# Splitting the down weights on ScalarE and VectorE instead of GpSimd in a nine-expert MoE kernel

## The reference, cut to what matters

```python
# x: 16 sequences x 128 tokens x 128 features, float32
def moe(h, gates, sg):                    # E=8 routed experts, F=512
    g = einsum('bsd,edf->ebsf', h, Wg)
    u = einsum('bsd,edf->ebsf', h, Wu)
    outs = einsum('ebsf,efd->ebsd', silu(g) * u, Wd)
    routed = einsum('be,ebsd->bsd', gates, outs)
    shared = (silu(h @ Sg) * (h @ Su)) @ Sd
    return (1 - sg) * routed + sg * shared
x = x + moe(x, ...)
x = x + layernorm(x + adapter(x, language)) * gamma[language] + beta[language]
```

## Time and profile before

| | us |
|---|---|
| median of three runs | 326.66 |
| fastest of them | 325.96 |
| span of the profiled execution (first to last instruction) | 324.8 |
| PE busy | 305.9 |
| DVE busy | 272.0 |
| ACT busy | 218.9 |
| POOL busy | 49.5 |

### The profile page before, as it was taken

The page is one execution under the profiler, slowest core; times in us unless marked ns, Lnnn a source line. Parts: engine busy times, 40 slices in busy tenths (PEclk is TensorE's granted clock), DMA queues, the critical chain, the costliest instruction groups (busy, mean ns, idle before and its releaser), DMA issues.

```text
span 324.8 us, 6936 instructions
## 1 busy us (share of the span) xinstructions
PE 305.9 (94%) x1397; PEld 139.4 (43%) x1397; DVE 272.0 (84%) x544; ACT 218.9 (67%) x471; POOL 49.5 (15%) x51
## 2 busy tenths in 40 slices
PE   5693969999999999999999999999999999999995
PEld 1231324444445444444445444444445444444443
DVE  3999999999986788898986788898986788898864
ACT  4573647888877677777777677777767677777540
POOL 2888894000001000000001000000001000100001
PEclk9799789999999999999999999999999999999996
DMA  6990233200000000000000000000000000000000
GB/s 209 414 387 13 38 80 77 69 0 2 1 0 0 14 4 0 0 1 0 0 32 0 12 4 0 0 0 0 0 32 1 12 4 0 1 0 0 0 32 32
DMA packets 9082, 11.97 MB, mean 37 GB/s; under 512 B 3810, under 2 KB 6770, under 8 KB 9074
## 3 DMA queue, kind: packets, MB, share of 16 engines
q1 hardware_dynamic: 8784, 11.68, 10.8%
q10 hardware_dynamic: 290, 0.20, 0.2%
HBM read 10.83 MB, written 1.05 MB: 37 GB/s over the span
## 4 chain that ended last, share of the span: by engine, by line
PE 85%; DVE 1%; issue 0%; DVEq 0%
PE moe_ps L272 9%; PE moe_ps L270 9%; PE moe_ps L269 9%; PE up_ps L227 9%; PE gate_ps L227 9%; PE up_ps L228 9%; PE up_ps L229 9%; PE gate_ps L228 9%; PE gate_ps L229 9%; PE back_ps L296 1%; PE adapt_ps L280 1%; PE x_ps L366 1%; PE x_ps L288 1%; PE x_ps L364 0%; DVE gx_lo L470 0%; PE gate_ps L357 0%
## 5 line engine op out<-in xcount | busy, mean ns | idle before, releaser
L391 ACT ACTIVATE silu<-gate_ps 128x512 f32<-128x512 f32 x144 | 85.7, 595 | 70.9 <-PE gate_ps L229 70.8
L487 DVE SCALAR_TENSOR_TENSOR hidden<-silu,up_ps 128x512 f32<-128x512 f32 x144 | 98.7, 685 | 36.5 <-PE up_ps L229 18.7
L493 DVE TENSOR_TENSOR h_lo<-hidden,h_hi 128x512 f16<-128x512 f32 x144 | 101.0, 702 | 0.1
L398 ACT ACTIVATE h_hi<-hidden 128x512 f16<-128x512 f32 x144 | 89.6, 622 | 15.6 <-DVE hidden L487 15.5
L227 PE MATMUL up_ps<-gx_hi,w_hi 128*128 (+1 forms) x142 | 54.5, 384 | 9.6 <-DVE gx_lo L470 7.0
L470 DVE SCALAR_TENSOR_TENSOR gx_lo<-x_full,coef,gx_hi 128x128 f32 (+3 forms) x144 | 57.4, 421 | 0.0
L272 PE MATMUL moe_ps<-h_lo,w_hi 128*128 128x512 f16 x144 | 55.1, 383 | 0.0
L270 PE MATMUL moe_ps<-h_hi,w_lo 128*128 128x512 f16 x144 | 55.1, 383 | 0.0
L269 PE MATMUL moe_ps<-h_hi,w_hi 128*128 128x512 f16 x144 | 55.0, 382 | 0.0
L227 PE MATMUL gate_ps<-x_hi,w_hi 128*128 (+1 forms) x142 | 54.6, 385 | 0.0
L228 PE MATMUL up_ps<-gx_lo,w_hi 128*128 (+1 forms) x142 | 54.5, 384 | 0.0
(11 more groups left out here) (90 smaller groups left out, 202.3 us busy)
## 6 DMA issues: line engine op xcount, KB each, us to landing
w_full<-weights SPq DMA_DIRECT2D x8, 768.0 KB, 13.3
affine_sb<-affine SPq DMA_DIRECT2D x16, 128.0 KB, 3.0
w_full<-weights SPq DMA_DIRECT2D x3, 256.0 KB, 5.5
x_full<-xT SPq DMA_DIRECT2D x1, 768.0 KB, 8.7
out_dram<-result SPq DMA_DIRECT2D x3, 256.0 KB, 2.1
w2b_sb<-w2b SPq DMA_DIRECT2D x16, 16.5 KB
x_full<-xT SPq DMA_DIRECT2D x1, 256.0 KB, 4.7
w_sb<-w SPq DMA_DIRECT2D x16, 16.0 KB
```

Of the source, the lines that this page charges most:

```text
L391: nc.scalar.activation(cols(silu, f % 2, N), gate_ps[f % 2][:, :], ACT.Silu, scale=1.0 / W_SCALE).then_inc(silu_ready, 1)
L398: nc.scalar.activation(cols(h_hi, f, N), cols(hidden, f % 2, N), ACT.Copy).then_inc(h_hi_ready, 1)
L487: nc.vector.scalar_tensor_tensor(out=cols(hidden, f % 2, N), in0=cols(silu, f % 2, N), scalar=HIDDEN_RESCALE, in1=up_ps[f % 2][:, :], op0= ...
L493: nc.vector.tensor_tensor(cols(h_lo, f, N), cols(hidden, f % 2, N), cols(h_hi, f, N), ALU.subtract).then_inc(h_lo_ready, 1)
```

## The change

ScalarE makes the high half and VectorE the low half of the down weights too, in the step f=2 of the expert ahead (`f < 3`), and those of expert 0 ahead of the first step. GpSimd's part and its two buffers go. The counts of the semaphores `w_hi_ready` and `w_lo_ready` go from two to three for an expert. The loads, TensorE's order and everything after tile 0 stay.

```diff
--- before.py
+++ after.py
-        down64 = sb("down64", [P, F], F32)
-        w_scale = sb("w_scale", [P, F], F32)
...
@@ gate_up, down (PE)
-                    pe.wait_ge(w_lo_ready, 2 * e + 1)
+                    pe.wait_ge(w_lo_ready, 3 * e + 1)
...
-                    pe.wait_ge(w_lo_ready, 2 * e + 2)
+                    pe.wait_ge(w_lo_ready, 3 * e + 2)
...
-                    pe.wait_ge(w_down_ready, e + 1)
+                    pe.wait_ge(w_lo_ready, 3 * e + 3)
@@ expert (ACT)
-                    if next_w is not None and f < 2:
+                    if next_w is not None and f < 3:
                         if f == 0:
                             act.wait_ge(experts_loaded, next_w)
                         weight_hi(next_w, f)
...
             act.wait_ge(w0_loaded[1], 16)
             weight_hi(0, 1)
+            act.wait_ge(w0_loaded[2], 16)
+            weight_hi(0, 2)
             expert(0, 0, True, 1, None)
@@ weight_lo, expert (DVE)
-                dve.wait_ge(w_hi_ready, 2 * e + third + 1)
+                dve.wait_ge(w_hi_ready, 3 * e + third + 1)
...
-                    if next_w is not None and f < 2:
+                    if next_w is not None and f < 3:
                         weight_lo(next_w, f)
...
             weight_lo(0, 1)
+            weight_lo(0, 2)
             for q in range(BATCHES):
                 gated_x_lo(0, 1, q)
@@ (POOL)
-            nc.gpsimd.memset(w_scale[:, :], W_SCALE).then_inc(w_scale_ready, 1)
...
-            def down_weight_parts(e):
...
-            pool.wait_ge(w_scale_ready, 1)
-            pool.wait_ge(w0_loaded[2], 16)
-            down_weight_parts(0)
-            with pool.Fori(1, NE) as e:
-                pool.wait_ge(experts_loaded, e)
-                pool.wait_ge(w_down_ready, e)
-                down_weight_parts(e)
             pool.wait_ge(x_rest_loaded, 16)
```

More of the change, by code:

```diff
@@ L120, in build @@
         warm_ready = sem("warm_ready")
[L121 to L124, removed]
         w0_loaded = [sem(f"w0_loaded{i}") for i in range(3)]
```

## The result

The changed kernel takes 314.38 us (median, 314.03 to 314.89) against 326.66 us of before; the ratio is 0.962, 95% interval 0.960 to 0.964, so 3.8% faster. A fourth execution of before took 644.2 us and is left out as an outlier. The prediction was 314.5. The profiled execution took 314.35 us with a span of 312.5, 12.3 less than before.

The account below looks back on a forecast made before the run. Tile 0 was taken as short of VectorE, later tiles of TensorE. 11.5 + 6.2 + 23.6 + 2.3 = 43.6 to expert 4; 0.4 lost after left 12.2 us gained: span 312.6, plus 1.86 gives 314.5 us, range 311.0 to 319.5.

Parts of the forecast that it names:

- The start: Beginning of tile 0: first `hidden` of expert 0 at 11.5 instead of 14.21, a gain of 2.7 us.
- Expert 0 to 3: VectorE in tile 0: 6.2 us for expert 0, then three experts at 7.88, together 23.6 us.
- the input split: GpSimd's conversions for tiles 1 to 3, moving from 45 us to about 11.8, still cost a full VectorE 2.3 us.
- The upper bound of 5.5: Most that GpSimd's input conversions could cost, in us, if they block all of VectorE's work.
- The third split: VectorE's added `w_lo` in each expert of the loop: 0.60 us, bounds 0.55 and 1.65.
- The period of 7.88: VectorE's us per expert in the loop: 7.14 busy, 0.14 for the branch, and the third `w_lo`; TensorE needs 7.77.
- PE waits these 0.1 us at f=0: Experts 4 to 7: PE waits for the last `gx_lo`, pushed back by the new `w_lo`; 0.4 us lost in all.
- C: Rival, tile 0: VectorE's long instructions have another cause than GpSimd and stay long; slower, 333.7 us; chance 0.03.
- A: Rival, tile 0: TensorE's clock drops again, three unhidden slow stretches cost 4.5 us; 319.0 us; chance 0.16.
- B: Rival, tile 0: VectorE's 7.88 is too high and PE runs through without a wait; 311.4 us; chance 0.07.
- to the letter: Port lock read strictly: all of GpSimd's input conversions stand in VectorE's way, 3.2 us more than the sum.

Follow-up runs that it names:

- the run without any split: Changed kernel with no split of the down weights on any engine, TensorE multiplying by the up weights in their place: 312.52 us.
- memsets: Changed kernel with nine rounds of seven write-only memsets on GpSimd ahead of its input split: 315.41 us, from 313.65 to 317.05.
- GpSimd's rounds: Changed kernel with GpSimd's old nine rounds on the down weights added, into spare buffers that nobody reads: 333.40 us.
- the best kernel: Changed kernel with third `w_lo` behind last `gx_lo`, tile 1's inputs split after the last weights, tiles 2 and 3's in tile 1: 311.26 us.
- the three runs on it: Changed kernel with GpSimd's old rounds added (333.40 us), with memsets in their place (315.41 us), with one-input casts in their place (326.79 us).
- late inputs: Changed kernel with GpSimd's split of the input of tiles 1 to 3 held back until VectorE's last low half of the weights: 312.09 us.

## Why the prediction was right, and which term was not

**What bounds the kernel** was right: only tile 0 changed, by 12.5 us at its end (95.25 to 82.77), and the later tiles kept their 216.0 us.

**The start** came out as walked: forecast 11.5, measured 11.49. The added split of expert 0 pushed ScalarE's second four `gx_hi` to 9.92, and VectorE's new `w_lo` lay in the wait for them: without both, in the run without any split, these `gx_hi` start at 9.51 and the first `hidden` at 11.08, each 0.41 earlier.

**Expert 0 to 3**: forecast for the three experts of the loop 23.6 us, measured 23.64 (19.72 to 43.36). Expert 0 with the input split was put at 6.2 + 2.3 = 8.5 and took 8.23; without it 6.12 (memsets). So the split costs 2.1 there, not 2.3; at 45 us in the memset run it costs 2.3. The upper bound of 5.5, in which every conversion stands fully in VectorE's way, was far off. The timeline shows why: beside the conversions three `w_lo` and three `h_lo` take 0.87 to 1.09 us where 0.68 is their length alone, which is 2.1 us in all, and each `hidden` between them keeps its 0.68.

**The third split** was priced at 0.60 and cost that: VectorE's busy time for an expert went from 7.14 to 7.74 us.

**The period of 7.88** was right as a number and wrong in its reason. The step that failed is the one that took 0.14 us between experts for the branch, as time "in which VectorE waits for nobody". Some 0.1 of it is a wait for TensorE's up product, which itself waits for the last `gx_lo`; moving the third `w_lo` behind that `gx_lo` took it away with the loop's branch still there (a gap of 0.03). The kernel before had the same wait in the very gap that was read as the branch:

```profile
54.61 0.34 DVE L470 SCALAR_TENSOR_TENSOR gx_lo<-x_full,coef,gx_hi 128x128 f32 x1
```

```profile
55.33 0.39 PE L227 MATMUL up_ps<-gx_hi,w_hi 128*128 x1
...
55.77 0.38 PE L229 MATMUL up_ps<-gx_hi,w_lo 128*128 x1
```

The third pass ends at 56.15 and the `hidden` of the earlier trace rows starts at 56.29, 0.14 later, just as 35.48 is 0.14 after 35.34 in the changed kernel. So the gap that was added to the sum held a wait that comes back after the change; that it kept its length made the number right, which is luck. Hence also the slip in "PE waits these 0.1 us at f=0": true, but VectorE then waits for PE in turn. The same edit, which by my sum would win nothing in the loop, won 1.2 us of last `hidden`: about 0.1 in each expert of the loop, and 0.6 once, TensorE's wait near 26 us, which fell from 1.54 to 0.94. VectorE's landmarks show that second part only in expert 8, which takes 7.33 us instead of 7.90. The prediction had waits of 0.1 us for `gx_lo` and not this one of 1.5.

**The rivals.** C priced a third split among stretched instructions at 333.7; that state was made with GpSimd's rounds, and took 333.4. The two numbers agree by luck: C left the first `hidden` at 14.21 and added 6.6 us in the experts 0 to 3, while that run starts at 16.81 and adds 2.6 in them. It needed GpSimd's reads, which is why it wasn't the changed kernel's. A (clock drops that cost 4.5 us) did not come about between 14 and 80 us: the granted clock is 1.00 there. The waits of over 3 us were gone, and the longest one left is 1.5 us, which no drop followed. B (311.4, PE without waits) is what the best kernel reaches at 311.26, though not for B's reason alone.

**The rule of the Trainium skill** ("SBUF — State Buffer", the two separate sides) that VectorE and GpSimd share a port pair as an exclusive lock, and that a VectorE instruction with two SBUF inputs meets it only against a GpSimd instruction that reads SBUF, agrees with the kernel before and the three runs on it: rounds with reads of one or two tensors stretch `w_lo` to 1.07 and 1.33 us, memsets leave it at 0.68, and `hidden` with one SBUF input stays at 0.68 beside all of them. So the prediction's reading of this rule "to the letter", as 3.2 us more, was too strict: by the rule's own exception `hidden` goes on beside a conversion, and only the instructions with two inputs wait.

## What to carry to other kernels

When VectorE is short and GpSimd works beside it on SBUF data, compare the durations of VectorE's two-SBUF-input instructions with and without GpSimd; what GpSimd costs them (here 14 us) can be far more than the work costs on VectorE itself (here 1.9 us). What stays on GpSimd goes where VectorE idles. And when TensorE waits for a result of VectorE and VectorE then waits for TensorE's product in turn, put that result ahead of work that nobody waits for, even if the sum of work is the same.

## What was not expected

**A VectorE result reaches TensorE 0.37 to 0.42 us after its instruction ends.** `gx_lo` ends at 34.10, the matmul starts at 34.52; before, 32.61 and 32.98. The round trip at each expert's end contains this time.

**The clock row can miss the first microseconds.** In the changed kernel PE spaces its matmuls 0.43 us apart until 12.8, its lower level of 1.2 GHz, yet the window of 12 to 16 us and the one of 8 to 12 show a granted clock of 1.00. Timeline of PE and its window:

```profile
11.07 0.63 PE L245 MATMUL up_ps<-gx_hi,w_hi 128*128 128x512 f16 x1
11.50 0.63 PE L247 MATMUL up_ps<-gx_lo,w_hi 128*128 128x512 f16 x1
11.92 0.63 PE L249 MATMUL up_ps<-gx_hi,w_lo 128*128 128x512 f16 x1
```

```profile
12.00:16.00 4.00, 4.00 (x17) 1.00 1.02 418
```

In the second profile of the same kernel the row does show it, 0.50 from 8 to 11 us, and the spacing is back at 0.22 from 11.2 on. It cost nothing: the first `hidden` of expert 1 starts at 19.72 in one and 19.73 in the other. The spacing of the matmuls tells the level more surely than the row.

**The last 13 us vary by more than some of these effects.** From the last `hidden` to the end of the span it takes 13.7 us in the changed kernel, 12.8 with late inputs, and 14.4 in the best one, with the same instructions. TensorE's clock drops in that tail at one place or another: its row is at 0.67 for 304 to 312 us in the changed kernel and at 0.50 in the best one. That the place of the drop makes the difference was not tested. So edits worth a microsecond in tile 0 were read at the last `hidden`, which repeats within 0.02 us (298.80 and 298.82).
